# Splitting the routed layer's tokens nine groups to seven instead of eight to eight, and moving the scatter, the routing and two edges of the schedule with it

## The reference

```python
x = x + xattn0(layernorm(x), ctx)        # q = x W.T + b; softmax(q ctx.T) ctx
x = x + moe(layernorm(x))
x = x + xattn1(layernorm(x), ctx)        # q, k, v projections, 1/sqrt(128)
x = x + trees(layernorm(x))              # 8 trees of depth 7

def moe(x):
    logits = x @ gate_w                  # 8 experts
    top_val, top_id = max(logits), argmax(logits)
    xs = x * sigmoid(top_val)
    routed = swiglu(xs, expert[top_id])  # one expert per token
    return swiglu(x, shared) + routed
```

## Time and profile before

| | us |
|---|---|
| three runs, median (lowest, highest) | 867.29 (867.15, 867.87) |
| the profiled execution, its own time | 868.49 |
| its span, first to last instruction | 866.7 |
| PE busy | 794.8 (92%) |
| DVE busy | 653.7 (75%) |
| ACT busy | 539.0 (62%) |
| POOL busy | 272.3 (31%) |
| mean granted TensorE clock | 0.976 |

### The profile page before, as it was taken

The page is one execution under the profiler, slowest core; times in us unless marked ns, Lnnn a source line. Parts: engine busy times, 40 slices in busy tenths (PEclk is TensorE's granted clock), DMA queues, the critical chain, the costliest instruction groups (busy, mean ns, idle before and its releaser), DMA issues.

```text
span 866.7 us, 15372 instructions
## 1 busy us (share of the span) xinstructions
PE 794.8 (92%) x4488; PEld 639.0 (74%) x4489; DVE 653.7 (75%) x1728; ACT 539.0 (62%) x944; POOL 272.3 (31%) x341
## 2 busy tenths in 40 slices
PE   5999996877769958999999999999999999999997
PEld 3788885766569958987777777777777777777775
DVE  5788887866585527669888888988888888888774
ACT  2577675554223313437777776877777777768765
POOL 1332331488437717013213222321331232121000
PEclk8999999999799979999999999999999999999999
DMA  6346773533314424210000000000000000000000
GB/s 147 95 119 193 204 211 106 169 102 97 110 49 146 145 76 113 80 50 13 19 7 25 24 0 24 24 24 1 24 24 15 9 24 24 0 24 13 13 1 25
DMA packets 91426, 55.72 MB, mean 64 GB/s; under 512 B 13439, under 2 KB 88183, under 8 KB 91255
## 3 DMA queue, kind: packets, MB, share of 16 engines
q1 hardware_dynamic: 74304, 40.38, 16.6%
q0 software_dynamic: 4096, 8.40, 3.4%
q10 hardware_dynamic: 12983, 6.41, 2.7%
HBM read 32.10 MB, written 23.07 MB: 64 GB/s over the span
## 4 chain that ended last, share of the span: by engine, by line
PE 34%; DVE 22%; ACT 13%; issue 12%; POOL 12%; DMA 4%; ACTq 1%; DVEq 1%; POOLq 0%; SPq 0%
POOL x_sorted L507 5%; PE PS L758 4%; DVE sil_l L1446 4%; DVE dec L1430 3%; DVE xn_c L1090 3%; PE PS L1009 3%; POOL rs L492 3%; PE PS L1011 3%; PE PS L1010 3%; PE PS L773 3%; ACT sil L715 2%; PE PS L1031 2%; PE PS L1033 2%; PE PS L1032 2%; ACT L715 2%
## 5 line engine op out<-in xcount | busy, mean ns | idle before, releaser
L715 ACT ACTIVATE sil<-PS,b_in_c 128x512 f32<-128x512 f32 x256 | 162.2, 686 | 113.3 <-PE PS L1018 108.3
L1446 DVE TENSOR_TENSOR sil_l<-sil,sil_h 128x512 fp32r<-128x512 f32 x256 | 164.7, 684 | 44.7 <-ACT sil_h L723 44.2
L490 POOL TENSOR_TENSOR ve<-mv,eps 128x4 f32<-128x4 f32 x64 | 17.6, 276 | 458.4 <-DVE mv L1084 458.3
L723 ACT ACTIVATE sil_h<-sil 128x512 fp32r<-128x512 f32 x224 | 128.9, 631 | 0.0
L1031 PE MATMUL PS<-sil_h,wout_l 128*128 128x512 f32 x256 | 117.2, 458 | 1.6 <-DVE sil_l L1446 1.6
L1430 DVE TENSOR_SCALAR dec<-PS,b_in_c 128x512 bf16<-128x512 f32 x128 | 95.4, 746 | 26.2 <-PE PS L1011 26.2
L1009 PE MATMUL PS<-x4T_h,win_l 128*128 128x512 f32 x256 | 102.2, 399 | 2.0 <-ACT yo L675 0.7
L1033 PE MATMUL PS<-sil_h,wout_h 128*128 128x512 f32 x256 | 100.4, 392 | 0.0
L1032 PE MATMUL PS<-sil_l,wout_h 128*128 128x512 f32 x256 | 100.4, 392 | 0.0
L1011 PE MATMUL PS<-x4T_h,win_h 128*128 128x512 f32 x256 | 99.9, 390 | 0.0
L1010 PE MATMUL PS<-x4T_l,win_h 128*128 128x512 f32 x256 | 99.9, 390 | 0.0
(11 more groups left out here) (165 smaller groups left out, 1564.2 us busy)
## 6 DMA issues: line engine op xcount, KB each, us to landing
x_sorted<-zeros SPq DMA_DIRECT2D x4, 1280.0 KB, 6.8
xs_in<-x_sorted SPq DMA_DIRECT2D x20, 256.0 KB
y_sorted<-yo ACTq DMA_DIRECT2D x20, 256.0 KB, 2.5
X<-in_x SPq DMA_DIRECT2D x16, 256.0 KB, 2.8
rows<-xn SPq DMA_DIRECT2D x16, 256.0 KB, 2.5
xs<-rows SPq DMA_DIRECT2D x16, 256.0 KB, 3.0
out<-res SPq DMA_DIRECT2D x16, 256.0 KB, 2.4
ctxT<-in_ctx_t SPq DMA_DIRECT2D x16, 240.0 KB, 3.2
```

The source lines that it names most:

```text
L715: act.activation(tile(sil[p % 2], c, W), bank(2 * (p % 2) + c), ACT.Silu, bias=b_in_c[:, 2 * p + c:2 * p + c + 1]).then_inc(t_silu, 1)
L723: act.activation(tile(sil_h[p % 2], c, W), tile(sil[p % 2], c, W), ACT.Copy).then_inc(t_hi, 1)
L1446: dve.tensor_tensor(tile(sil_l[p % 2], c, W), tile(sil[p % 2], c, W), tile(sil_h[p % 2], c, W).bitcast(F32), ALU.subtract).then_inc(t_lo, 1)
```

## The change

Four things are changed together.

1. **The split.** The first part has 9 groups and the second 7 (HGS), so the first part has 44 tiles or 11 units, the second 36 tiles or 9 units; there are still 20 units.
2. **The scatter.** It has four buffers `xs` (XB) instead of two. A call scatters 128 rows with its index straight from POS; a group's scaling (`scale`) takes its scores straight from SCORE, and stands in the middle of the four calls of the group before it, so the four calls after it are not those that need it. In stage A the 36 calls of the first part are spread over bodies 13 to 18 by the table CALLS, each body's share before and after the second `rstd`.
3. **Routing by quarters.** `a_choose` works on up to four groups (QUADS) and is spread over more bodies. Counting, first slots and slots of the first part all stand in body 12. ACT reads the counts there, and ACT copies `probT` out in bodies 11 to 13. The triangle of ones has 1 taken off everywhere, which saves the subtraction in `a_slots`. The second part's choosing is done in bodies 16 and 18, and only three groups of it in body 18.
4. **Edges.** LATE_W goes by SP's queue. The first merge of weights, the first KT and DVE's casts and splits move from body 0 to body 1. In stage R some steps of the early attention move by one unit, or from behind a unit into it.

```diff
+XB = 4
...
-HB = B // HALVES
-HG = NG // HALVES
-HTILES = HB + E
...
-HR = NR // HALVES
+HGS = (9, 7)
...
+HG = HGS[0]
...
+HR = HRS[0]
+MB, MT = HBS[0], HTILES[0]
+QUADS = ((0, 4), (4, 4), (8, 1), (9, 4), (13, 3))
...
-    before = np.triu(np.ones((P, P), np.float32), 1)
+    before = np.triu(np.ones((P, P), np.float32), 1) - 1.0
...
-        ROUTES = {HG + 2: "choose", HG + 3: "count", HG + 4: "place", NG: "pack", NG + 2: "all"}
+        ROUTES = {HG - 1: "choose0", HG + 1: "choose1", HG + 2: "choose2", HG + 3: "count", NG: "pack", NG + 2: "all"}
+        SCATTER_FROM = HG + 4
+        CALLS = [0, 6, 12, 18, 25, 32, 36]
...
-                     (k, k + 1) if 0 <= k < HG else (), ROUTES.get(f))
...
-        FIRST_EARLY = HR + 2
+                     range(CALLS[k], CALLS[k + 1]) if 0 <= k < len(CALLS) - 1 else (), ROUTES.get(f))
...
+        def turned_by_act(g):
+            return HG + 1 <= g <= HG + 3
...
+        FIRST_EARLY = HR + 1
...
+            for dst, src in LATE_W:
+                sp.dma_start(dst, src).then_inc(w_late, 16)
...
+                    for k in range(XB):
+                        load_rows(k)
+                if g == HG + 4:
+                    load_rows(4)
+                if g == HG + 5:
+                    load_rows(5)
+                    load_rows(6)
+                if g == HG + 6:
+                    load_rows(7)
...
+            load_rows(8)
+            all_scattered(sp, HG)
...
-            with sp.Fori(HR // 2 - 1, NR // 2 - 1) as i:
+            for k in range(HG, HG + XB):
+                load_rows(k)
+            for r in range(HR - 2):
+                r_next(r, r % 2, 0)
+                if r > 2 and HG + XB + r - 3 < NG:
+                    load_rows(HG + XB + r - 3)
+            all_scattered(sp, NG)
+            r_next(HR - 2, 1, 1)
+            with sp.Fori(HR // 2, NR // 2 - 1) as i:
                 for u in range(2):
...
-            def scale_rows(k, v, i):
-                pool.wait_ge(k_in[v], 16 * (i + 1))
-                pool.tensor_copy(idx[:, v, :], cols(POS, k * G, G))
-                pool.tensor_copy(sco[:, v, :], cols(SCORE, k * G, G)).then_inc(k_idx, 1)
-                pool.wait_ge(k_idx, k + 1)
+            def scale(k):
+                v = k % XB
+                pool.wait_ge(k_in[v], 16 * (k // XB + 1))
                 pool.tensor_tensor(by_tile(xs[v]), by_tile(xs[v]),
-                                   sco[:, v, :].unsqueeze(2).to_broadcast([P, G, P]), ALU.mult).then_inc(k_scaled, 1)
-            def scatter(k, v, h):
-                pool.wait_ge(k_scaled, k + 1)
+                                   SCORE[:, k * G:(k + 1) * G].unsqueeze(2).to_broadcast([P, G, P]),
+                                   ALU.mult).then_inc(k_scaled, 1)
+            def scatter(t, h, end):
+                v = (t // G) % XB
+                if t % G == 2 and t // G + 1 < end:
+                    scale(t // G + 1)
+                pool.wait_ge(k_scaled, t // G + 1)
                 pool.sem_inc(pool_passed, 1)
-                for j in range(G):
...
+                pool.indirect_dma_start(x_sorted[h], bass.IndirectOffsetOnAxis(ap=POS[:, t:t + 1], axis=0),
+                                        tile(xs[v], t % G), None).then_inc(scattered[v], 16)
...
+                if calls and calls[0] == 0:
+                    pool.wait_ge(zeroed, 16 * 4)
+                    pool.wait_ge(scored, 1)
+                    scale(0)
+                    pool.wait_ge(placed, 1)
+                half = (len(calls) + 1) // 2
+                for t in calls[:half]:
+                    scatter(t, 0, HG)
...
-                    scatter(units[1], 1, 0)
+                for t in calls[half:]:
+                    scatter(t, 0, HG)
...
+            pool.wait_ge(scored, 2)
+            scale(HG)
             pool.wait_ge(placed, 2)
-            pool.wait_ge(scored, 2)
-            with pool.Fori(0, HG // 2) as i:
-                for v in range(2):
-                    k = 2 * i + HG + v
-                    scale_rows(k, v, HG // 2 + i)
-                    scatter(k, v, 1)
+            for t in range(B0[1], B):
+                scatter(t, 1, NG)
...
-            for weights, done in ((FIRST_W, w_id), (ATT_W, w_att), (LATE_W, w_late)):
+            for weights, done in ((FIRST_W, w_id), (ATT_W, w_att)):
...
+                    if g is not None and turned_by_act(g):
+                        act.wait_ge(a_pT_ps, g + 1)
+                        act.activation(probT, bank(1, W, KEYS), ACT.Copy).then_inc(a_pT, 1)
+                    if route == "count":
+                        act.wait_ge(r_cnt, 1)
+                        act.activation(et(counts), by_tile(COUNTS_IN[0][1], E).rearrange("p t e -> p e t"), ACT.Copy)
+                        act.activation(ahead, COUNTS_IN[0][0], ACT.Copy).then_inc(r_read, 1)
...
+                if first(g):
+                    merge_weights()
+                    pe.wait_ge(m_done, 1)
+                    pe.matmul(bank(0, KW), WM[:, :], ctxT[0], start=True, stop=True).then_inc(a_k1_ps, 1)
+                elif f is not None:
+                    project_keys(f, u)
...
                     i.then_inc(a_pv_ps, 1)
+                if route == "count":
+                    pe.wait_ge(a_k0, f + 1)
+                    a_count(0)
...
-                    if r == FIRST_EARLY + 1:
-                        c_turn_x(0)
+                    if r == FIRST_EARLY + 3:
+                        c_scores(0)
+                    if r == FIRST_EARLY + 4:
+                        c_turn_prob(0)
...
                 now, coming = r_body(r, r % 2, now, coming)
                 if r == FIRST_EARLY + 2:
-                    c_scores(0)
-                if r == FIRST_EARLY + 3:
-                    c_turn_prob(0)
+                    c_turn_x(0)
...
+                    if not turned_by_act(g):
+                        dve.wait_ge(a_pT_ps, g + 1)
+                        dve.tensor_copy(probT, bank(1, W, KEYS)).then_inc(a_pT, 1)
...
+                if route == "count":
+                    dve.wait_ge(r_read, 1)
+                    a_first_slots(0)
                 if l is not None:
                     dve.wait_ge(s_sil, l + 1)
                     dve.tensor_tensor(s_act, s_act, PS[:, 6 * 512:8 * 512], ALU.mult).then_inc(s_act_d, 1)
-                if route == "choose":
-                    a_choose(0)
+                if route in ("choose0", "choose1", "choose2"):
+                    a_choose(int(route[-1]))
                 if route == "count":
-                    a_first_slots(0)
-                if route == "place":
                     a_slots(0)
                 if route == "pack":
+                    a_choose(3)
                     a_pack(0)
-                if first(f):
-                    take_merged()
+                if first(g):
                     cast_constants()
                     split_shared()
...
-                if r == FIRST_EARLY:
+                if r == FIRST_EARLY + 1:
                     c_rows3(0)
...
-                if r == FIRST_EARLY:
+                if r == FIRST_EARLY + 2:
                     c_norm3(0)
```

More of the change, by code:

```diff
@@ L575, in _ @@
             c_body(0, 0, 0)
-            for half, start, end in ((0, 0, HG // 2 - 2), (1, HG // 2 - 2, NG // 2 - 2)):
-                with pool.Fori(start, end) as i:
-                    c_body(2 * i + 1, 1, half)
-                    c_body(2 * i + 2, 0, half)
+            with pool.Fori(0, 2) as i:
+                c_body(2 * i + 1, 1, 0)
+                c_body(2 * i + 2, 0, 0)
+            c_body(5, 1, 0)
+            c_body(6, 0, 1)
+            with pool.Fori(3, NG // 2 - 2) as i:
+                c_body(2 * i + 1, 1, 1)
+                c_body(2 * i + 2, 0, 1)
             for g in range(NG - 3, NG):
@@ L633, in a_body @@
                     act.activation(cols(V, f * W, W), bank(3, W, KEYS), ACT.Copy).then_inc(a_v, 1)
[L634 to L638 removed]
+                if f is not None and not first(f):
+                    evac_keys(f)
+                if route == "count":
+                    score(0)
                 if route == "all":
@@ L1269, in a_choose @@
[L1269 to L1277 removed]
+                dve.wait_ge(a_lg, q + 1)
@@ new lines, in a_slots @@
+                up, sl, ah, ld, oh = (a[:, 0:n * E] for a in (upto, slot, ahead, lead, onehot))
+                step(dve.tensor_tensor(et(sl), et(up), first_slot.unsqueeze(2).to_broadcast([P, E, n]), ALU.add))
+                step(dve.tensor_tensor(te(ld), te(ah), sl.rearrange("p (e t) -> p t e", e=E), ALU.add))
+                step(dve.tensor_tensor(ld, ld, oh, ALU.mult))
+                step(dve.tensor_reduce(posf[:, 0:n], te(ld), AX.X, ALU.add))
+                dve.tensor_copy(POS[:, B0[h]:B0[h] + n], posf[:, 0:n]).then_inc(placed, 1)
```

326 lines of the change are left out of this document (159 added, 167 removed).

## The result

The changed kernel took 856.61 us (median of four runs, 856.13 to 858.12) against 867.58 us before: a ratio of 0.9879, 95% interval 0.9867 to 0.9891. The forecast was 849.7, the range 844 to 857. The direction was right, and 6.9 us of the forecast gain are missing. The profiled execution has 858.12 us and a span of 856.3, against 868.49 and 866.7 before.

The account below looks back on a forecast made before the run. Limits: PE in stages A, R and trees, POOL's first scatter, and a 10.18 us hole in stage R. Terms -1.5 - 5.4 - 11.8 + 1.1 = -17.6 on 868.49 give 850.9; the median, 1.2 lower, is 849.7 us, range 844 to 857.

Parts of the forecast that it names:

- The start: First bodies: seven loads moved to SP and the first maximum put ahead of the casts gain 2.9 us, between 0 and 4.6.
- the cover that might be missing: First bodies: casts cost nothing if done about when the second group's scores end; otherwise up to 2 us of gain goes.
- The routing: Bodies 10 to 12: the routing's extra time falls from 11.2 to 9.2 us, a gain of 2.0, bounds -2 and +5.
- The first scatter: Stage A: 67.5 us to the last call's start at 228.0; first unit's turn at 233.2, 1.5 us earlier.
- The start of stage R: First to fourth turn: 26.17 us becomes 20.8, 5.4 less, as 6.5 us of DVE work fits PE's idle time.
- The start of stage R stays as long: Rival: silu, slots and the pack are a chain by themselves, so no gain there: 855 us, chance 0.07.
- The hole: Stage R, before the twelfth unit: PE's standstill vanishes with 13 us to spare, gaining 10.2 us plus 1.6 of slow clock.
- the early attention: Stage R from body 15: scores in mid-body cost 1.9 us, the first norm saves 0.8; net +1.1, bounds -1 and +3.
- What is late next is PE itself: Stage R: once the hole is gone, PE, no longer the second scatter's data, is the late one.
- The per-call wait: Scatter calls: each call's own wait and semaphore step may cost nothing or 0.63 us; the forecast took nothing.
- The slow rival: Rival: each scatter call costs 0.63 us more for its wait and semaphore step: 876 us, chance 0.05.
- this lock: Shared VectorE and GpSimd port: if some 28 DVE copies each blocked a call, the second scatter would take 12.9 us longer.

Follow-up runs that it names:

- before_itself: The kernel before the change, unedited, run again for its trace: 867.12 us, ratio 0.9995.
- all_ahead_2: Changed kernel with last group's remaining work, counts' products, ACT's score and DVE's second-part slots before the first unit's turn: 849.80 us; 858.09 and 858.87 with late PE signals.
- attention_2: Changed kernel with stage R's early attention back in the old kernel's order on PE, ACT and DVE: 862.27 us; 869.37 in a series with late PE signals.
- changed_again: The changed kernel itself, unedited, run again in a series with late PE signals: 867.49 us, ratio 1.0003 to the kernel before.
- disturbed traces: Traces from three of five series, where some PE signals arrive up to 3 us late in stage R; the unedited changed kernel took 867.5 us there.
- scatter2_at_turn6: Changed kernel with POOL's second scatter held until PE has turned the sixth unit's rows: 871.94 us, ratio 1.0063, with late PE signals.
- the 8 and 8 kernels: Changed kernel with parts of 8 and 8 groups instead of 9 and 7, without and with last-group work moved before the first turn: 843.04 and 843.31 us.
- all_ahead_8_8: Changed kernel with parts of 8 and 8 groups and the last group's work and second-part routing moved before the first unit's turn: 843.31 us, ratio 0.9715.

## Why the prediction was right in direction and wrong in size

**The start: right in mechanism, half hidden in its own trace.** Forecast 2.9, in the two profiled executions 1.2 up to body 3, by the medians of all traces 2.8. ACT's first table load is at 5.27 us instead of 8.64 and the first maximum at 13.11 instead of 14.76. Two things stand in that trace against the rest; neither was tried alone. The casts stand ahead of the second group's maximum (23.29 us, its scores done at 22.06), which the prediction named as the cover that might be missing. And PE ran body 2's first products at the slow clock:

```profile
26.50:30.00 3.50, 3.50 (x10) 2.77 (x11) 3.02 (x7) 0.27 (x1) 2.30 (x3) 0.53 0.10 31
```

Eight products took 3.3 us there and 1.9 before. Where the first maximum comes a microsecond sooner as well, body 3 starts at 36.6 to 37.4, 2.5 to 3.2 before the profile of before. But before_itself, with the old start, has 38.49 too, so that a part of the 1.2 as of the 2.9 is the scatter from one execution to the next.

**The routing: right.** Bodies 8 to 12 hold 8.75 us beyond plain ones (1.75, 2.3, 1.5 and 3.2 in bodies 8, 10, 11 and 12) where there were 11.2: 2.4, forecast 2.0.

**The first scatter: right, with some luck.** Last call at 228.25 against 228.0, first turn at 233.46 against 233.2. The stretch to the last call took 66.6 us (from 161.66) where 67.5 were forecast, and it began 1.2 later than forecast: two misses that cancel.

**The start of stage R: the step that failed.** "This 6.5 us of work now fits into PE's idle time before the turn, because the turn is set by POOL and not by DVE." The time was there, 13.06 us, and all_ahead_2 shows the work in it. But PE executes in program order, and the turn that waits stood ahead of the last group's work. I had read the order on POOL and SP and took for granted that PE and DVE "reach this point sooner". PE's last product before the turn did end sooner (220.4, before 234.1), but nothing of the last group's could follow it. And I wrote that PE's restart is slow and gave it no term here; it took 2.3 us (three products at a granted clock of 0.52). Instead of -5.4 the term is +1.1, 6.5 us off, which is nearly all of the 6.9 that are missing. With the order moved on PE, ACT and DVE the time is 849.80 against a forecast of 849.7; that it is so close is luck, since POS then comes at 230.29 and not at 241.7. Of the prediction's own rivals, "The start of stage R stays as long" (855, given 0.07) is the one that came true, with its reason in part: silu, slots and pack are a chain, but here it also started late, since PE's counts stood behind the turn.

**The hole and the early attention: size right, reasons half wrong.** From the fourth turn to the tree stage -10.4, forecast -10.7. PE's wait behind the scores (1.90 us at 348.57, forecast 1.9) and the missing wait for `rs` are as forecast, but not what they add up to. "What is late next is PE itself" holds only because the change also adds the gathered rows a unit later; with the whole old order, that wait included, 5.9 us come back (attention_2), so the +1.1 is charged to a move without which the kernel would be 5.9 us slower. And 14 us of spare time for the second scatter should have raised the question whether the split was needed: it cost 13.4 us and saved none. The forecast gave the hole's 11.8 us to the split and the calls together. It charged the split with the four calls and the scaling more of the first scatter, but not with the body (11 us) by which that scatter could start earlier without it; against the kernel before, which starts it at the same body, this doesn't show.

**The per-call wait: right, it costs nothing.** The slow rival has no support in any trace.

The sum then reads -3.8 (start and routing up to body 13), +2.5 (to the first turn), +1.1, -10.4, +0.2: -10.4, where the forecast had -4.9, +3.4, -5.4, -10.7 and 0: -17.6.

## What to carry to other kernels

An idle gap of an engine takes in only the work that stands ahead of the waiting instruction in that engine's own program, and in the program of each engine that work passes through: before counting a gap as cover, read the order at its edge. When a long wait disappears, look for what ran inside it, since a later stage's inputs are now asked for that much earlier. A change made of several parts should be priced part by part: here one of them (9 and 7) cost more than the whole gained.

## What the runs showed of the hardware

**Late PE signals.** In changed_again, at one turn, PE, ACT, SP and DVE:

```profile
287.43 0.60 PE L809 MATMUL PS<-WA,xs_in 128*128 128x128 f32 x4
```

```profile
291.07 0.60 ACT L630 ACTIVATE xsT<-PS 128x512 f32<-128x512 f32 x1 [3.91 <-remote]
```

```profile
291.06 6.53 SPq L479 DMA_DIRECT2D xs_in<-x_sorted  x2
```

```profile
290.85 0.69 DVE L1438 TENSOR_TENSOR ract<-sg,PS 128x512 f32<-128x512 f32 x1 [3.20 <-PE PS L1010]
```

The turn ends at 288.03, and normally ACT starts 0.04 us later. Here ACT and SP, which wait for the same semaphore, and DVE, which waits for a product begun at 287.86, all go on 3 us later within 0.2 us of each other. In the disturbed traces such lags (up to 3.1 us) lie between 250 and 303 us, while POOL issues the second scatter; in scatter2_at_turn6, where it runs from 271 to 313, they lie between 290 and 314. Another of some 1.05 stands at unit 16 in all of them but attention_as_before. The bodies of stage A beside the first scatter are not longer. In the disturbed series the changed kernel takes 11 us more and all_ahead 8 to 9; the kernel before took 866.2 to 867.6 us in all five series. Whether its 10 us wait hides them was not seen, since its trace was taken in undisturbed series only. One chip gave both kinds in different series. The cause stays open, and the 8 and 8 kernels were only measured undisturbed.

**POOL's scaling holds DVE up.** DVE in all_ahead_8_8, then POOL:

```profile
224.82 0.29 DVE L1329 TENSOR_TENSOR lead<-LG,top 128x128 f32<-128x128 f32 x1
225.15 1.17 DVE L1330 TENSOR_TENSOR lead<-lead,c_rout 128x128 f32<-128x128 f32 x1
```

```profile
225.14 1.03 POOL L531 TENSOR_TENSOR xsa<-xsa,SCORE 128x512 f32<-128x512 f32 x1 [11.28 <-ACT SCORE L632]
```

An instruction with two inputs from SBUF takes 1.17 us instead of 0.29 when POOL's scaling starts with it, and ends right behind it. In the changed kernel `expert_f` took 1.77 us instead of 0.20 beside the scaling at 251.80, on the path of the product that PE begins at 256.16. The prediction weighed this lock only in the other direction, DVE's copies against POOL's calls. The Trainium skill (SBUF — State Buffer, section "SBUF: two separate sides") says that whichever of the two starts first keeps the pair for its whole instruction, and names a DVE instruction with two SBUF inputs as one that takes part; these rows agree; for `expert_f`, which began at 251.14, the call ahead of the scaling (250.82 to 251.78) would have had it first, which no row shows apart.
